# A fused Mamba-2 and attention block over eight inputs: statistics three units earlier, norm powers moved, scan operands padded, unread products added

## What is computed

```python
xn = _layernorm(x, axis=-1)
s = _L0_attn_ref(xn, ...)          # layer norm, Mamba-2 scan (4 heads of 64, 64 states), MLP with gelu
g = _silu(_L0_ffn_ref(xn, ...))    # rms norm, causal attention (16 heads of 8), top-2 of 4 experts
x = x + s * g
```

## Time and profile before

| | |
|---|---|
| median of 3 runs | 913.11 us (911.67 to 915.75) |
| the profiled execution | 912.75 us |
| span of its instructions | 911.0 us |
| mean granted TensorE clock | 0.967 |
| TensorE (PE) busy | 796.8 us, 87% |
| VectorE (DVE) busy | 632.1 us, 69% |
| ScalarE (ACT) busy | 502.1 us, 55% |
| GpSimd (POOL) busy | 300.3 us, 33% |

### The profile page before, as it was taken

The page is one execution under the profiler, slowest core; times in us unless marked ns, Lnnn a source line. Parts: engine busy times, 40 slices in busy tenths (PEclk is TensorE's granted clock), DMA queues, the critical chain, the costliest instruction groups (busy, mean ns, idle before and its releaser), DMA issues.

```text
span 911.0 us, 17953 instructions
## 1 busy us (share of the span) xinstructions
PE 796.8 (87%) x5396; PEld 473.8 (52%) x5396; DVE 632.1 (69%) x1491; ACT 502.1 (55%) x960; POOL 300.3 (33%) x566
## 2 busy tenths in 40 slices
PE   3549999998999889998999899998999989998887
PEld 1324454745547455654546455464556546464545
DVE  1675468784888748885697847886588856977523
ACT  2324675465843675456754667436754567446552
POOL 4322606044231614135150542316151351405300
PEclk9756999999999999999999999999999999999979
DMA  4000000000000000000000000000000000000000
GB/s 157 1 8 12 15 1 1 8 14 24 0 1 6 25 11 0 7 12 24 0 0 7 13 23 0 1 17 24 0 0 7 12 24 0 0 7 13 24 0 12
DMA packets 15144, 11.72 MB, mean 13 GB/s; under 512 B 1040, under 2 KB 13968, under 8 KB 14992
## 3 DMA queue, kind: packets, MB, share of 16 engines
q1 hardware_dynamic: 15120, 11.43, 4.2%
HBM read 7.76 MB, written 2.10 MB: 11 GB/s over the span
## 4 chain that ended last, share of the span: by engine, by line
PE 56%; DVE 17%; issue 12%; ACT 8%; POOL 6%; DVEq 1%; POOLq 0%; ACTq 0%
PE R L443 38%; PE S L443 13%; DVE sb_mx L1176 6%; DVE sb_x L1422 2%; POOL sb_pr L1690 2%; POOL sb_lnv L1595 2%; PE S L448 1%; DVE sb_tokqk L1359 1%; PE R L561 1%; PE R L448 1%; ACT sb_es L1114 1%; ACT L943 1%; ACT sb_junk L989 1%; DVE sb_st L1200 1%; DVE sb_yc L1480 1%
## 5 line engine op out<-in xcount | busy, mean ns | idle before, releaser
L1079 ACT ACTIVATE sb_pr<-S 128x768 f32<-128x768 f32 (+1 forms) x192 | 165.6, 887 | 152.3 <-PE S L443 151.2
L1176 DVE TENSOR_REDUCE sb_mx<-S 128x2 f32<-128x256 f32 (+3 forms) x256 | 198.0, 817 | 37.8 <-PE S L443 35.7
L1690 POOL TENSOR_SCALAR_AFFINE_SELECT sb_pr<-sb_pr 128x256 f32<-128x256 f32 (+1 forms) x192 | 97.0, 507 | 339.6 <-ACT sb_pr L1079 337.6
L443 PE MATMUL R<-sb_pr,sb_va 128*32 128x512 f32 (+3 forms) x1024 | 89.7, 445 | 19.6 <-POOL sb_pr L1690 19.6
L443 PE MATMUL S<-sb_maskb,sb_identb 128*128 128x128 bf16 (+1 forms) x384 | 51.4, 249 | 32.8 <-DVE sb_mx L1176 30.2
L443 PEld LDWEIGHTS S<-sb_maskb,sb_identb 128*128 128x128 bf16 x384 | 27.8, 101 | 100.3 <-DVE sb_mx L1176 83.6
L443 PE MATMUL R<-sb_xfT,sb_W 128*128 128x512 f32 x144 | 75.9, 635 | 3.3 <-ACT sb_pr L943 3.3
L443 PE MATMUL R<-sb_W,sb_pr 128*128 128x96 f32 (+1 forms) x512 | 70.9, 279 | 0.0
L443 PEld LDWEIGHTS R<-sb_W,sb_pr 128*128 128x128 f32 x512 | 62.8, 192 | 4.4 <-issue 3.6
L443 PE MATMUL S<-sb_kT,sb_qT 32*128 32x256 f32 (+3 forms) x512 | 58.9, 403 | 0.0
L443 PE MATMUL S<-sb_qT,sb_kT 32*128 32x256 f32 (+3 forms) x512 | 57.2, 388 | 0.0
(11 more groups left out here) (208 smaller groups left out, 1712.3 us busy)
## 6 DMA issues: line engine op xcount, KB each, us to landing
sb_xin<-x SPq DMA_DIRECT2D x9, 256.0 KB, 2.8
sb_W<-weights SPq DMA_DIRECT2D x1, 2290.0 KB, 10.5
sb_qT<-sb_mT SPq DMA_DIRECT2D x128, 4.0 KB
sb_xres<-x SPq DMA_DIRECT2D x8, 256.0 KB, 2.9
out<-sb_xres SPq DMA_DIRECT2D x7, 256.0 KB, 2.3
sb_cT<-sb_xact SPq DMA_DIRECT2D x8, 128.0 KB, 2.3
sb_W<-weights SPq DMA_DIRECT2D x1, 514.0 KB, 5.1
sb_cst<-consts SPq DMA_DIRECT2D x1, 328.0 KB, 3.2
```

Of the source, the lines that this page charges most:

```text
L443: return pe.matmul(o, lhsT, rhs, start=start, stop=stop, skip_group_check=True)
L1079: act.activation(pr[:, e % 4, :, 0:n], S[pair_of_exp(e)][:, :, 0:n], ACT.Exp).then_inc(p_sb, 1)
L1176: o = dve.tensor_reduce(mx[:, n // P - 1, g, heads[0]:heads[1] + 1], found[:, :, at_col:at_col + n], AX.X, ALU.max, negate=True)
L1690: pool.affine_select(out=keep, in_=keep, compare_op=ALU.is_ge, fill=0.0, base=0, pattern=pattern, channel_multiplier=-1)\
```

## The change

Five things are changed. The statistics move from unit 11 to unit 8, and the three GpSimd steps go behind the selects of units 11, 13 and 17 instead of 12, 13 and 16. `norms` thereby goes from unit 17 to unit 18; nothing of VectorE stands between the two places. `cT` and `hst`, operands of the scan with 64 rows, become tiles of 128 rows whose lower half is set to zero once by two GpSimd memsets at the start, and the two kinds of products that read them run over 128 rows. TensorE's start waits for two more of GpSimd's signals. `dense(o, n)` issues n products of the identity with 256 columns of constants whose results nobody reads: four or three behind each of the nine parts of the first `stage_b` (30 in all), and one, four, two and one in the last `stage_b` (eight), which also gets two waits at its start for the banks they write. The loop gets no such product.

```diff
-STATS_AT = 11
-NORM_AT = (12, 13, 16)
+STATS_AT = 8
+NORM_AT = (11, 13, 17)
...
-        cT = sb("cT", [NS, L])
+        cT = sb("cT", [P, L])
...
-        hst = sb("hst", [NS, DI])
+        hst = sb("hst", [P, DI])
...
-                    sp_e.dma_start(cT[:], xact[NS:2 * NS, 2, :]).then_inc(c_moved, 16)
+                    sp_e.dma_start(cT[0:NS, :], xact[NS:2 * NS, 2, :]).then_inc(c_moved, 16)
...
-                mm(R[2][:, 3 * P:4 * P], xact[0:NS, 2, s], cT[:, s]).then_inc(xt_ps, 1)
+                mm(R[2][:, 3 * P:4 * P], xact[:, 2, s], cT[:, s]).then_inc(xt_ps, 1)
...
+            def dense(o, n):
+
+                for _ in range(n):
+                    mm(o, ident, cst[:, 0:256])
+
             def stage_b(r, tail, head):
+                if tail and not head:
+                    pe.wait_ge(mx_sb, at(mx_sb, r, 0))
+                    pe.wait_ge(p_sb, at(p_sb, r, 0))
...
                     transposes(R[0], lambda t: ao[:, t, :]).then_inc(aoT_ps, 1)
+                    if not head:
+                        dense(bank(0)[:, 0:256], 1)
...
                     i.then_inc(wo_ps, 1)
+                    if not head:
+                        dense(bank(0)[:, 0:256], 4)
...
                     transposes(R[1], lambda t: x1n[:, t, :]).then_inc(x1T_ps, 1)
+                    if not head:
+                        dense(bank(0)[:, 0:256], 2)
...
                     transposes(R[0], lambda t: xf[:, t, :]).then_inc(xfT_ps, 1)
+                    if not head:
+                        dense(bank(0)[:, 0:256], 1)
...
                         max_scores_of_four(r, g, part)
+                        if not tail:
+                            dense(R[0][:, 0:256], 4 if part == 0 else 3)
...
-            pe.wait_ge(pool_set, 8)
+            pe.wait_ge(pool_set, 10)
...
-                    dve.tensor_copy(hst[:], R[1][0:NS, 0:DI]).then_inc(h_sb, 1)
+                    dve.tensor_copy(hst[0:NS, :], R[1][0:NS, 0:DI]).then_inc(h_sb, 1)
...
+            pool.memset(cT[:], 0.0).then_inc(pool_set, 1)
+            pool.memset(hst[:], 0.0).then_inc(pool_set, 1)
             for step in range(3):
                 first_norms(-2, step)
```

More of the change, by code:

```diff
@@ L1492, in scan_state @@
                 if c == 0:
-                    dve.tensor_copy(hst[:], R[1][0:NS, 0:DI]).then_inc(h_sb, 1)
+                    dve.tensor_copy(hst[0:NS, :], R[1][0:NS, 0:DI]).then_inc(h_sb, 1)
                 else:
                     tt(hdec[:].rearrange("p (h d) -> p h d", h=NH),
-                       hst[:].rearrange("p (h d) -> p h d", h=NH),
+                       hst[0:NS, :].rearrange("p (h d) -> p h d", h=NH),
                        dec[0:NS, 2, c, :].unsqueeze(2).broadcast_to([NS, NH, HP]),
@@ L1499, in scan_state @@
                     dve.wait_ge(h_sb, at(h_sb, r, 2 * c))
-                    tt(hst[:], R[1][0:NS, 0:DI], hdec[:], ALU.add).then_inc(h_sb, 1)
+                    tt(hst[0:NS, :], R[1][0:NS, 0:DI], hdec[:], ALU.add).then_inc(h_sb, 1)
             def stage_a(r, tail):
```

## The result

| | before | after |
|---|---|---|
| median, runs on the same chips | 913.35 us (6 runs) | 888.64 us (6 runs) |
| all times of after | | 880.93, 881.20, 888.07, 889.21, 890.51, 890.57 us |
| ratio | | 0.970 [0.965, 0.974] |
| the profiled execution | 912.75 us | 880.93 us (span 879.1 us) |

The kernel became faster by 24.7 us, where 28.8 were forecast. The time after lies inside the range, 4.3 us above the predicted 884.3. But the six times fall into two groups, near 881 and near 889, with nothing between, and the profiled execution is one of the first group: it gained 31.8 us. So two questions are open after the result: what brings more than 28.8 us in the one group, and what takes 8 us back in the other.

The account below looks back on a forecast made before the run. TensorE was taken as the bound, with time won only where it waits or runs slowly. Terms -19.6 + 1.6 - 1.6 - 3.7 - 2.0 - 4.2 + 0.7 = -28.8 us gave 884.3 us; range 877.5 to 895.

Parts of the forecast that it names:

- order of statistics and norm powers, net: stage_a passes: TensorE's 16 waits on GpSimd's select vanish, -19.6 us, against +1.6 us for a later ao.
- padding: Scan products over 128 rows: 0.12 us gained per product, 0.2 us a pass booked, 1.6 in all, bounds 0 and 6.7.
- first `stage_b` and the stretch behind: Unread products hold the clock at 1.00: 3.7 us gained in the parts, 2.0 in the stretch behind.
- last `stage_b`: Unread products keep the clock at 1.00, so transposes, gate product and experts' first products take 4.2 us less.
- memsets at the start: Two GpSimd memsets before the first norms lie on the path to the first product: 0.7 us added.
- few tenths: Most given back when TensorE, before unit 16's scores, waits for ScalarE to finish unit 15.
- The delay of `ao`: At unit 9, statistics moved to unit 8 make ao later: 0.2 us a pass, 1.6 lost, bounds 0 and 2.4.
- the row at 58%: Window 861.0 to 864.5 us before the change: clock 1.00 with TensorE 58% busy, taken as evidence the clock would hold.
- (d): Unit 8: VectorE reaches the statistics before xin lands, delaying ao and TensorE; 929 us if landing takes 12 us; chance 0.03.
- (b): A norm power meets another select, at unit 12 or 18, giving back half of 19.6 us: 894 us; chance 0.10.
- (a): Unread products don't hold the clock in one or both stage_b places: 888 to 900 us; chance 0.17.
- (c): More gain than booked: padding counts fully or the stretch behind the first stage_b does: 876 to 882 us; chance 0.08.

Follow-up runs that it names:

- (5): The base with statistics and norm steps back at units 11 and 12, 13, 16: 898.49 us, ratio 0.985.
- (4): The kernel before with only the statistics at unit 8 and norm steps at 11, 13, 17: 892.77 us, ratio 0.978.
- (6): The base with the two scan products over 64 rows again, memsets kept: 885.62 us, ratio 0.970.
- (7): The base without the 30 unread products of the first stage_b: 886.21 us, ratio 0.971.
- (8): The base without the eight unread products of the last stage_b: 884.03 us, ratio 0.969.
- experiment 1: The changed kernel run again, no edit: 887.78 us, ratio 0.972 to the kernel before; profiled execution 890.99 us.
- 2: The changed kernel with VectorE's gate weights one step later (WEIGHTS_FROM 7 instead of 5): 880.26 us, ratio 0.964.
- (9): The base with norm step 0 back behind unit 12, the others left at 13 and 17: 884.69 us, ratio 0.969.
- the base: The changed kernel with WEIGHTS_FROM = 7 instead of 5, the kernel most follow-ups edit: 880.26 us, ratio 0.964.
- experiment 11: The base with four more unread products, around the end of the first stage_b and the last head group's first scores: 878.05 us, ratio 0.963.
- (10): The base with the first stage_b's 30 unread products over 32 rows instead of 128: 890.71 us, ratio 0.977.
- Experiment 12: The base with one unread product a part in the first stage_b instead of four or three: 885.59 us, ratio 0.971.
- experiment 3: The kernel before with only WEIGHTS_FROM = 7: 911.55 us against 912.55, ratio 1.000.

## Why the prediction came out as it did

| step | forecast | measured |
|---|---|---|
| order of statistics and norm powers, net | -18.0 | -18.2 (5), -19.8 (4) |
| padding | -1.6 | -5.4 (6), of it 3.4 in loop and end; about -4 without the smaller meeting |
| first `stage_b` and the stretch behind | -5.7 | -6.0 (7) |
| last `stage_b` | -4.2 | -3.8 (8), of it 3.0 in the last stage |
| memsets at the start | +0.7 | +0.6 (wait for `xa` 13.1 to 13.7) |
| GpSimd's long operations meeting VectorE's short ones | not in the sum | +7.5 to +8.4 in the median (1, 2) |

**The order: the waits went as said, and the net is right partly by luck.** Both waits went. The free time before the select of unit 12 was there. That before the select of unit 18 was not: from the end of unit 17's select (202.64) to the end of its exponentials (204.45) are 1.8 us, not the 3.1 that were taken over from unit 12, and the long step takes 3.0. The select came 1.15 us late, and no loss came of it, as TensorE needs it only at 206.51. The prices were off too, in ways that cancel. What was to be late next came as said, a wait for ScalarE before the scores of unit 16, but it is 0.54 us a pass, 4.3 in all, above the "few tenths", and stood in the sum at nothing. Against it, half of the waits for `ao` went (2.1 to 2.4 us) where they were to stay, and the 1.6 us booked for a later `ao` didn't come. The sentence "the place left at unit 11 gives nothing back by itself" was wrong: with the statistics early the power behind unit 12 leaves a wait of 0.7 us in place of 1.5 and costs 4.4 us at most (9), so leaving unit 11 was worth about half of the first stall. The delay of `ao`, booked at 0.2 us a pass, is not to be seen: the wait for it at unit 9 is 0.29 us as before.

**Padding: mechanism right, size too low.** The row pair that was read (0.48 us for two, 0.36 expected) gave 0.12 us a product; it measured 0.10. But only 0.2 us a pass were taken, with the argument that three of the four `scan_inputs` stand before scores whose consumer is busy. The passes say 0.36 beside the smaller meeting of the base and 0.5 without it. The argument holds, as part of the gain comes back as 4.3 us of waits, but it was priced too high, and the prediction missed that the neighbour gets faster too (0.71 to 0.61). The term, booked at 1.6 us, measured 3.4 in loop and end, about 4 without the smaller meeting, within the bounds of 0 and 6.7; 1.7 us of the difference lie in the start, where the clock's return is chance.

**Unread products: right.** The clock held from 38 to 67.8 us and, in the result's trace and the base's, at the end; in experiment 1 it fell there for 3.5 us. It fell for 6.7 us behind the first `stage_b`, the place that the prediction named as doubtful and booked at 2.0 of 4.7 us; experiment 11 has the 2 us that were left there. The step that argued with busy time alone ("over 75%" against the row at 58%) came to the right answer by an incomplete measure: with 32 rows TensorE was busy 18.5 of 18.5 us at 0.50 (10). Experiment 12, where the clock fell too, doesn't speak against it: its products would be some 7 of 18.5 us at full clock, less than in the row at 58%.

**What was missing.** Without it the forecast would have been too high: the parts bring 3.5 us more than booked, and the base stands at 880.3. The meeting takes 7.5 to 8.4 us back in the median. The prediction had seen a row of this kind, the select of 0.88 us beside VectorE, and put it aside as lengthening a step, not the order. That is the step that failed. It also named the sentence of the Trainium skill that GpSimd shares its interfaces to the SBUF with VectorE ("GPSIMD Engine Reference", section 1, Specifications). It left out the condition that stands there: contention with VectorE's instructions in a 2-port mode or with two inputs in the SBUF. The traces agree as far as they go: the products and comparisons that were held up have two such inputs, and the reciprocal at 248.23 with one was not (0.18 us). The prediction thought of VectorE slowing GpSimd, at the norm powers. It didn't ask the reverse question, which long GpSimd operation starts close to a short VectorE operation on the path, in the part of the pass that the change doesn't touch. There the distance was 0.03 to 0.04 us in all seven passes of the loop. That the median lies only 4.3 us from the forecast is luck: an under-sized and a missing term point opposite ways. Of the rivals, (d) did not come about, (b) did at unit 18 but cost nothing, (a) only for the 6.7 us behind the first `stage_b`; (c) did in part: the base, at 880.3, lies in its 876 to 882, and the padding that counts for more is one of its two reasons.

Two things are open. The order and the padding together bring GpSimd's steady lead, and the order alone brings it in one pass, but by which operation the lead arises was not followed. And why an execution of the changed kernel settles in one group or the other was not found; one of each group was traced.

## What to carry to other kernels

When a change shortens a loop, look at the pairs of operations of VectorE and GpSimd elsewhere in it that start within a few tenths of each other: one of two operands and 64 columns behind one of 512 takes the long one's time, and a time that comes in two groups is a sign to look for it. Move one of the two by a step, and look at what the long one meets then: here it was a smaller operation with more room behind it, 0.2 us a pass in place of 1.3. It is only worth doing where the meeting exists, as experiment 3 shows. Unread products paid here where TensorE idled in short gaps at half clock, with three or four of 128 rows in each gap and shorter than it; with one in each nothing came back, and with 32 rows less than nothing. Before a few us are put down to an edit, compare where the clock rose in the start of the two traces.

## What was not expected of the hardware

- A VectorE operation of two operands and 64 columns (0.21 us) that began 0.04 us behind a GpSimd operation of two operands and 512 columns ended with it: it took 1.31 us, and 0.96 us for the next pair. One of 16 columns is held as well (1.01 us in place of 0.17); a reciprocal of one operand under the same GpSimd operation is not (0.18). The other way round, a GpSimd product of 16 columns took 0.63 us in place of 0.22 beside a VectorE tap, and a power of 4 columns 1.54 in place of 1.03 where VectorE worked beside it.
- A product over 64 rows between ones over 128 cost about 0.10 us for itself and 0.10 for the next; its weight load is no shorter (184 against 192 ns).
- In two executions of one kernel, with the same work on TensorE, the clock returned to 1.00 at 33.6 and at 35.7 us, and the first `xin` of the loop was issued 1.7 us apart.
- The granted clock didn't follow busy time alone: it was 1.00 at 15.8 of 18.5 us busy with 128 rows, and 0.50 at 18.5 of 18.5 with 32 rows in the added products.
